# A decoder layer with routed experts on one core: the last tile's product in float32, both halves of a tile put together, the router's steps in another order, and the slot weights in another bank

## The reference

```python
x = x + attn(layernorm(x), ...)      # 16 heads; weights (eps + distance(Q, K)) ** -2, normalised; gated by G
x = x + xattn(layernorm(x), ctx, ctx, mask, ...)   # softmax attention over 77 context rows
x = x + ffn(layernorm(x), gate_w, rms_w, W1, W2, W3)
...
def ffn(x):                          # 8 experts, the best two of each token
    y = rmsnorm(x, rms_w)
    vals, idx = top_k(y @ gate_w.T, 2)
    w = softmax(vals)
    h = silu(y @ W1[e].T) * (y @ W2[e].T)       # 704 hidden values
    return x + sum over the two experts e of w[e] * (h @ W3[e].T)
```

## Time and profile before

| what | value |
| --- | --- |
| median of 3 runs | 1432.39 us (1429.56 to 1433.23) |
| the profiled execution's own time | 1428.5 us |
| its span (first to last record) | 1426.4 us |
| busy TensorE, VectorE, ScalarE, GpSimd | 89%, 79%, 73%, 50% of the span |
| mean granted TensorE clock | 0.95 of full speed |

### The profile page before, as it was taken

The page is one execution under the profiler, slowest core; times in us unless marked ns, Lnnn a source line. Parts: engine busy times, 40 slices in busy tenths (PEclk is TensorE's granted clock), DMA queues, the critical chain, the costliest instruction groups (busy, mean ns, idle before and its releaser), DMA issues.

```text
span 1426.4 us, 23505 instructions
## 1 busy us (share of the span) xinstructions
PE 1263.9 (89%) x7513; PEld 865.1 (61%) x7513; DVE 1132.7 (79%) x1569; ACT 1036.4 (73%) x839; POOL 708.7 (50%) x524
## 2 busy tenths in 40 slices
PE   5899999999999999999998955999993699999992
PEld 4545554554455455545544714888873599999992
DVE  7988998898889889888988473788886867777771
ACT  1699999999999999999999931333332356666661
POOL 5456656665665666566655152333330245565642
PEclk9999999999999999999999767999995799999996
DMA  5000000000000000000000124222220134334422
GB/s 156 5 11 16 30 15 29 15 22 22 15 29 15 29 15 29 15 29 15 15 22 0 28 76 130 85 67 66 66 98 15 31 91 123 76 97 98 101 30 74
DMA packets 69214, 67.78 MB, mean 48 GB/s; under 512 B 6816, under 2 KB 61600, under 8 KB 69152
## 3 DMA queue, kind: packets, MB, share of 16 engines
q1 hardware_dynamic: 61504, 56.91, 12.6%
q0 software_dynamic: 7680, 10.49, 4.4%
HBM read 49.29 MB, written 20.19 MB: 49 GB/s over the span
## 4 chain that ended last, share of the span: by engine, by line
PE 35%; ACT 19%; issue 19%; DVE 13%; DMA 7%; POOL 5%; POOLq 1%; DVEq 0%; ACTq 0%; SPq 0%
ACT wts L1586 11%; PE ps_s L577 8%; DMA acc<-norms,tok_put 6%; PE ps_o L593 6%; PE ps_o L666 4%; ACT wts L1588 4%; DVE wts L1046 3%; PE ps_p L488 3%; PE ps_o L879 2%; PE ps_s L699 2%; PE ps_s L727 2%; PE ps_s L846 2%; POOL head_rows L1864 2%; ACT L1583 1%; POOL tok_now L1861 1%
## 5 line engine op out<-in xcount | busy, mean ns | idle before, releaser
L1782 POOL TENSOR_TENSOR v_aug<-v_aug,wts 128x1024 f32<-128x1024 f32 x96 | 232.4, 2421 | 227.3 <-DVE v_aug L1035 226.9
L1046 DVE TENSOR_SCALAR wts<-ps_s,k 128x1024 f32<-128x1024 f32 x240 | 296.9, 1278 | 55.3 <-PE ps_s L577 51.9
L593 PE MATMUL ps_o<-wts,head_rows 128*64 128x512 f32 x1024 | 249.0, 610 | 3.6 <-ACT wts L1588 3.6
L1586 ACT ACTIVATE wts<-wts,eps_d 128x2048 f32<-128x2048 f32 (+1 forms) x96 | 246.0, 2562 | 0.2
L1580 ACT ACTIVATE wts<-wts 128x4096 f32<-128x4096 f32 (+1 forms) x80 | 230.1, 2931 | 21.0 <-DVE wts L1054 18.6
L1588 ACT ACTIVATE wts<-wts 128x2048 f32<-128x2048 f32 (+1 forms) x96 | 238.4, 2483 | 3.0
L577 PE MATMUL ps_s<-q_hi,k_hi 64*128 64x512 f32 x512 | 122.5, 471 | 34.0 <-DVE wts L1046 17.8
L593 PEld LDWEIGHTS ps_o<-wts,head_rows 128*64 128x64 f32 x1024 | 63.2, 137 | 128.0 <-issue 118.0
L1035 DVE TENSOR_TENSOR v_aug<-v_aug,wts 128x1024 f32<-128x1024 f32 x96 | 126.5, 1317 | 6.6 <-ACT wts L1588 6.2
L577 PEld LDWEIGHTS ps_s<-q_hi,k_hi 64*128 64x128 f32 x512 | 49.3, 185 | 103.4 <-DVE wts L1046 62.5
L577 PE MATMUL ps_s<-q_lo,k_hi 64*128 64x512 f32 x512 | 102.6, 392 | 0.0
(11 more groups left out here) (280 smaller groups left out, 3170.7 us busy)
## 6 DMA issues: line engine op xcount, KB each, us to landing
wts<-in_w SPq DMA_DIRECT2D x16, 704.0 KB, 5.5
raw<-in_w_in SPq DMA_DIRECT2D x64, 128.0 KB, 2.3
h_t<-o_step SPq DMA_DIRECT2D x16, 512.0 KB, 2.7
head_rows<-h_t SPq DMA_DIRECT2D x16, 512.0 KB, 4.4
wts<-in_w SPq DMA_DIRECT2D x8, 640.0 KB, 7.5
acc<-wts SPq DMA_DIRECT2D x17, 128.0 KB, 1.8
wts<-in_x SPq DMA_DIRECT2D x2, 1024.0 KB, 5.9
wts<-in_x SPq DMA_DIRECT2D x1, 2048.0 KB, 9.2
```

The lines of the kernel that those rows point to most:

```text
L593: mm = pe.matmul(ps_o[r, t], v_pair[:, b, r], wts[:, h, b, t], start=b == 0, stop=b == SB - 1)
L1046: dve.tensor_scalar(wts[:, h, b, :], ps_s[:, h, :], k2[:, 2 * b + h:2 * b + h + 1], 0.0, ALU.add, ALU.max).then_inc(S_.max_ok, 1)
L1586: act.activation(chunk(start, end), chunk(start, end), ACT.Ln, bias=eps_d[:, 0:1]).then_inc(S_.ln_ok, 1)
L1782: pool.tensor_tensor(acc_w[:, 0], acc_w[:, 0], wts[:, 0, b], ALU.add).then_inc(S_.add_ok, 1)
```

## The change

Four edits.

1. **The last tile's product.** `down_last` multiplies `h_all` by w3 as float32, with no high and low parts: 12 products of 256 columns instead of 36, in two parts by chunks of the hidden values, the two halves into two banks. The last tile drops `high_hidden`, `high_down`, `low_hidden` and `low_down`.
2. **Puts and gathers.** GpSimd copies both columns of the token table at once, and issues the two transfers of a tile behind each other. A put no longer waits, between its halves, for the first to land; it waits for both halves of the tile before. Empty slots of the two halves get different rows.
3. **The router's order.** The slots come first, both columns of pairs in one instruction; the one-hot matrices are finished for one column of pairs, then for the other, and TensorE starts on the first when it is ready; the table of the tiles comes last. Expert 0's weights are split without waiting for the table.
4. **Slot weights.** Their 32 products go to a bank of `ps_p`, behind `up_gate` 1 of tile 1, and the wait for `w_slot` stands behind `down` of tile 0 instead of ahead of it.

```diff
@@ TensorE
-            pe.wait_ge(S_.oh2_ok, 1)
             for r in range(2 * NT):
+                if r % NT == 0:
+                    pe.wait_ge(S_.oh2_ok, r // NT + 1)
                 mm = pe.matmul(ps_s[:, 0, 512:512 + 2 * ES], oh_lo[r // NT][:, r % NT],
...
+            def down_last(k):
+                banks = ps_o[:, 0:D], ps_o[:, HALF:HALF + D]
+                pe.wait_ge(S_.o_ok2, k)
+                for part, chunks in enumerate((range(0, 4), range(4, NC))):
+                    pe.wait_ge(S_.hm_ok, W_PIECES * k + 2 + part)
+                    for half in range(2):
+                        for j in chunks:
+                            r = slice(DEL, P) if j == NC - 1 else slice(0, P)
+                            mm = pe.matmul(banks[half], h_all[r, j, half * P:(half + 1) * P], w3_sb[r, (E - 1) % 2, j],
+                                           start=j == 0, stop=j == NC - 1)
+                        if part:
+                            mm.then_inc(S_.w3_mm, 1)
...
             def slot_weights():
+                pe.wait_ge(S_.hm_ok, W_PIECES)
                 for k in range(2):
...
-                        mm = pe.matmul(ps_o[:, HALF:HALF + 3 * ES], oh_lo[k][:, n], oh_w[k][:, :, n],
+                        mm = pe.matmul(ps_p[:, HALF + TT:HALF + TT + 3 * ES], oh_lo[k][:, n], oh_w[k][:, :, n],
...
+                up_gate(k, 1, n)
                 if n == 1:
                     slot_weights()
-                up_gate(k, 1, n)
                 if n >= 1:
-                    if n == 1:
-                        pe.wait_ge(S_.wslot_ok, 3)
                     down(k - 1, n - 1)
+                if n == 1:
+                    pe.wait_ge(S_.wslot_ok, 3)
                 up_gate(k, 2, n)
...
-            down(tiles - 1, 2)
+            down_last(tiles - 1)
@@ ScalarE
-            def copy_out(k, n):
+            def copy_out(k, n, last=False):
...
                 for half in range(2):
+                    at = half * HALF if last else HALF + half * D
+                    if last and half:
+                        act.wait_ge(S_.w3_mm, k + 2)
                     if n >= 1:
                         act.wait_ge((S_.os_even, S_.os_odd)[half], 16 * k)
...
-                high_hidden(k, 0, n)
+                if not last:
+                    high_hidden(k, 0, n)
                 silu(k, 2, n)
-                high_down(k, slot, n)
-                high_hidden(k, 1, n)
                 if not last:
+                    high_down(k, slot, n)
+                    high_hidden(k, 1, n)
@@ GpSimd
-            def put(k, par, first=False):
-
-                i = 2 * k + par
-                now = S_.put_first if first else (S_.put_even, S_.put_odd)[par]
-                pool.wait_ge(S_.o_ok2, i + 1)
-                if par:
-                    pool.wait_ge(S_.os_even, 16 * (k + 1))
...
+            def put_tile(nth):
+                if not (isinstance(nth, int) and nth == 1):
+                    for q in (S_.os_even, S_.os_odd):
+                        pool.wait_ge(q, 16 * (nth - 1))
+                pool.tensor_copy(tok_put[:], tok_i[:, bass.ds(2 * nth - 2, 2)]).then_inc(S_.put_ok, 1)
                 pool.wait_ge(S_.slot_ok, 1)
...
+                pool.wait_ge(S_.put_ok, nth)
+                pool.wait_ge(S_.o_ok2, nth)
+                for half, q in enumerate((S_.os_even, S_.os_odd)):
+                    pool.indirect_dma_start(out=acc, out_offset=bass.IndirectOffsetOnAxis(ap=tok_put[:, half:half + 1], axis=0),
+                                            in_=o_sb[:, half], in_offset=None, compute_op=ALU.add).then_inc(q, 16)
```

171 lines of the change are left out of this document (75 added, 96 removed).

## The result

The changed kernel takes 1393.69 us (median of 4 runs, 1392.61 to 1395.16), the kernel before 1432.08 us in the same measurement (median of 4, 1429.56 to 1433.23). The ratio of the two is 0.9735, with a 95% interval from 0.9718 to 0.9752: 2.65% faster. The forecast was 1399 us with a range of 1392 to 1411.

What follows compares the result with a forecast made beforehand. Bounds in four places: the router's thread of small steps, the wait for `w_slot`, late scatters in the loop, a serial end. 3.9 + 6.2 + 10.1 + 13.1 = 33.3 us off 1432.4 gives 1399 us; range 1392 to 1411.

Steps and rivals of the forecast that it cites:

- Router: In the router: slots 1.5 us earlier, overlapped token products 1.2, second gather 1.2 earlier; 3.9 us in sum.
- The wide steps: In the router: VectorE's product and sum of 256 columns on the way to `slot_i`, taken as 0.42 us each.
- Slot weights: Tile 1, ahead of `down` of tile 0: no wait for `w_slot`, products at full clock; 6.2 of 6.6 us counted.
- The part that hangs on the clock (2.0): In `down` of tile 0: 36 products at full clock take 4.66 us, not 6.7; 2.0 us gained.
- Loop: Tiles 0 to 18: no scatter waited for, TensorE's 13.01 us a tile sets the step; 10.1 us gained.
- Last tile: From tile 18's copy-out to the end: twelve float32 products in 5.6 us, scatters 1.6 apart; 13.1 us gained.
- That the loop stays at the scatters' pace: Rival, in the loop: paired scatters beside an expert's load land late, none of 10.1 us comes, 1409 us; chance 0.13.
- That the end stays at the low clock: Rival, last tile: float32 products at 1.2 GHz or scatters landing later together, 5.6 us less gain, 1405; chance 0.12.
- GpSimd held in the first gather: Rival, in the router: a late copy and two long issues take 2.5 us back, 1401.5; chance 0.08.
- The pair of scatters that slows itself: Rival "Slower", in the loop: paired scatters share 16 engines; 1437 us if a pair takes 12 us; chance 0.04.

Runs made afterwards that it cites:

- the one with merged gathers: The kernel before with both token columns copied at once and the two gathers issued behind each other, puts as before: 1418.71 us, ratio 0.9917.
- the kernel with the paired puts alone: The kernel before with both halves put at once, the gathers as before, each with its own copy: 1415.05 us, ratio 0.9878.
- the run with serial halves: The changed kernel with the two halves of a put in turn again, the gathers still merged: 1421.86 us, ratio 0.9959 to the kernel before.
- one experiment: The changed kernel with the last tile's float32 product waiting for all hidden values before its first product: 1396.02 us, ratio 0.9769 to the kernel before.

## Why the prediction was right, point by point

*Router.* Forecast 3.9, measured 3.97. The wide steps took 0.43 and 0.42, where I had taken 0.42. The pipelined token products gave what was said. Of the 1.2 us from the merged gathers 0.9 came between the issues and 0.3 behind, as the second issue took 0.96 us in place of 1.18. Edit 2 without the router's order gave 1.20 alone, the router's order without edit 2 2.76: the two parts add up.

*Slot weights.* Forecast 6.2 of a possible 6.6, measured 6.46, 5.98 alone. The part that hangs on the clock (2.0) was the doubtful one; it came, with the clock at 1.00 through `down` and no wait above 0.51 us ahead of it.

*Loop.* Forecast 10.1, measured 9.90, and by what was said: TensorE's own 13.0 us a tile. The forecast took both halves of the edit as one; the runs show that the paired puts do all of it in the loop. It had the path right on which the loss reaches TensorE (a held copy-out, the high and low parts, the next `down`), but it put the late scatter down to GpSimd's wait between the halves alone; in six of the seven cases it was also an expert's load that the second scatter fell into. It also counted 0.8 us on each side of a small copy; the rows have it only behind (a copy starts at 1256.99, where the issue before it ends).

*Last tile.* Forecast 13.1, measured 12.67. Off by small sizes: the products took 5.79 for 5.6, the second scatter started 1.86 behind the first, not 1.6 (an issue of 1.56 and 0.31 between). The Trainium skill, "FP8 and Floating Point Precision", on TensorE precision, has true float32 make four passes. The trace agrees with it better than I had it: in the loop 1828 records, nearly all of them float32r products of 256 columns, take 224.00 us, 0.12 each, and the two float32 products in the middle of the kernel took 0.47 each, nearly four times that; the twelve of `down_last` took 0.48 each. I had divided a whole `down`, with its start and end, by 36. So a float32 product does cost TensorE more than three float32r ones, 0.48 us against 0.36. At the full clock `down` of the last tile would take 4.66 us, less than the 5.79. The edit gains because it needs no splits ahead of it and so has neither the wait (5.66 us) nor the low clock behind it, not because it is less work. The 8.63 us of the kernel before came again in four of the five other kernels that keep this `down` (8.62 or 8.63), but the one with merged gathers had 6.62 behind the same wait; with that, the end would have gained 2 us less.

*The time itself.* The span's gain was forecast as 33.3 and came as 33.1; the profiled execution was to take 1395.2 us and took 1395.16. The median is off by 5.4 us, and the step behind it is the last one: I added the 3.9 us by which the median of the runs lay above the profiled execution, and took that for an offset. In the changed kernel the profiled execution lies 1.5 us above the median, and 3.9 + 1.5 = 5.4. Part of the spread may be the serial puts' own: the loops of that kind took 243.8 to 247.0 us in four profiles, those with paired puts 233.86 to 233.93 in eight. In one group nine runs of the kernel before had spans from 1425.4 to 1432.0 us, 6.6 apart, and five of the changed kernel 1392.0 to 1394.6, 2.6 apart. But that the paired puts took the spread of the whole away isn't shown: four runs of the kernel with the paired puts alone had spans from 1407.7 to 1413.8, 6.1 apart.

The range held in part by luck. Its lower end was to be the sum with its bounds and a run as fast as the profiled one, which is 1399.1 - 0.4 - 0.4 - 3.9 = 1394.4, and the sum by itself was to lie from 1394 on; no term stands for the rest down to 1392, and the median came at 1393.69.

*The rivals.* None of them came. That the loop stays at the scatters' pace: refuted by 224.00 of 224.00 us. But its condition never arose: in the changed kernel a load starts when a pair has landed, and at most its last 0.6 us lie beside the start of the next pair. Where a scatter does meet a load, as in the kernels with serial puts, it is waited for much longer: 7.2 us in the run with serial halves, 7.8 with merged gathers, 8.6 in the kernel before. That the end stays at the low clock: the clock was 1.00, but the 2.02 us wait of one experiment was enough to make the products 1.9 us longer, a third of the 5.6 that the rival had. GpSimd held in the first gather: its copy took 0.19 and the issues 1.21 and 0.96, beside VectorE's work on the table. The pair of scatters that slows itself: GpSimd waited for scatters in three tiles of 20, 2.5 us each, off the path, and the landings took 4.0 us at most.

## What to carry to other kernels

An engine that issues transfers in order is a bound by the length of its list, waits for landings included, and not by its busy share: GpSimd was busy for half of the span here, and yet its late transfers cost the loop half a microsecond a tile. Look for a landing that is waited for in the middle of such a list, and for small copies, each with a handover of 0.8 us behind it. Ask also what a transfer that is issued late will run into: here the second scatter, 5.3 us behind the first, met a load of 2 MB, and 1.9 us behind it met nothing. A wait of TensorE costs more than its length when the clock falls behind it, so cover it with products that can run already; and a wait for late data belongs behind the work that doesn't need it. When a profiled execution lies at one end of the runs, ask which stretch scatters before carrying the difference over to the changed kernel.

## What the runs showed that I had not expected

- A wait of 2.02 us ahead of the last products was enough for the clock to fall from 1.00 to 0.50 a moment after they had begun, although TensorE was busy all through by then; they took 7.70 us in place of 5.79.
- `down` of tile 0 behind the same wait of 5.25 us took 6.7 us in one kernel and 8.7 us in another (clock 0.50 through all of it), and the last `down` behind 5.66 us took 8.63 us in one and 6.62 in another: the same code and the same wait, 2 us apart.
- A scatter of 128 rows lands in 3.8 us at the median, but it was waited for until 7.2 to 9.0 us behind its start where an expert's weights loaded beside it, and the wait ended with the load. The two of a pair, with 0.3 us between the issues, don't disturb each other measurably: all 40 of the changed kernel landed in 3.6 to 4.0 us.
- Products of no use in TensorE's waits raised the clock as meant (second token group 0.85 in place of 1.46 us) and gained 1.7 us in place of 3.3, with VectorE next on the chain.
- The stretch ahead of the router, 1084 to 1088 us, varies by 4 us between profiles with the same instructions. Effects of a few microseconds show only between markers inside the trace.
